# Cross attention with a layer norm on one core: two diagonal Gram blocks packed into one operand, and the keys' mean from one product

## The reference, cut to what matters

```python
# x (4, 2048, 512), ctx (4, 77, 384), all fp32
text_p  = x @ W_text + b_text              # (4, 2048, 512)
audio_p = ctx @ W_audio + b_audio          # (4, 77, 512)
Q = layer_norm(text_p, g1, beta1)
K = layer_norm(audio_p, g2, beta2)
alpha = softmax(Q @ K^T / sqrt(512))
H = (alpha @ audio_p) @ W_out + b_out
out = layer_norm(H + x, g_out, beta_out)
```

## Time and profile before

| what | value |
|---|---|
| median of 3 runs | 277.38 us (276.97 to 277.71) |
| profiled execution, its own time | 277.88 us |
| span of the profiled execution, first to last instruction | 276.2 us |
| mean granted TensorE clock | 0.992 of full |
| busy: PE / DVE / ACT / POOL | 264.3 / 230.8 / 199.1 / 203.4 us |
| share of the chain that ended last: PE / DVE / DMA | 86% / 4% / 3% |

### The profile page before, as it was taken

The page is one execution under the profiler, slowest core; times in us unless marked ns, Lnnn a source line. Parts: engine busy times, 40 slices in busy tenths (PEclk is TensorE's granted clock), DMA queues, the critical chain, the costliest instruction groups (busy, mean ns, idle before and its releaser), DMA issues.

```text
span 276.2 us, 5994 instructions
## 1 busy us (share of the span) xinstructions
PE 264.3 (96%) x1705; PEld 240.3 (87%) x1705; DVE 230.8 (84%) x716; ACT 199.1 (72%) x509; POOL 203.4 (74%) x223
## 2 busy tenths in 40 slices
PE   6799999999999999999999999999999999999980
PEld 6579788999999999999999999999999999999830
DVE  3757889788888888888888888888888888888895
ACT  3584293257888887777777778888888888888881
POOL 5053400113699999999999999999999999999985
PEclk9999999999999999999999999999999999999996
DMA  6919794432244444444444444444444444454116
GB/s 188 285 53 303 277 345 159 120 105 77 77 154 152 157 152 153 154 152 153 152 153 152 152 152 153 153 152 152 152 152 154 153 152 152 152 153 148 81 77 266
DMA packets 21056, 44.03 MB, mean 159 GB/s; under 512 B 2114, under 2 KB 4750, under 8 KB 21034
## 3 DMA queue, kind: packets, MB, share of 16 engines
q1 hardware_dynamic: 20410, 42.74, 45.8%
q10 hardware_dynamic: 624, 1.06, 1.4%
HBM read 21.19 MB, written 16.78 MB: 138 GB/s over the span
## 4 chain that ended last, share of the span: by engine, by line
PE 86%; DVE 4%; DMA 3%; POOL 3%; ACT 2%; issue 1%; SPq 1%; POOLq 0%; ACTq 0%; DVEq 0%
PE psY L1268 44%; PE psO L1280 10%; PE psT L1193 10%; PE psY L1258 7%; DMA zs<-in_ctx_dram 3%; PE psE L1243 2%; PE psE L1244 2%; PE psY L1098 2%; PE psY L1162 1%; PE psT L1131 1%; PE psT L1162 1%; POOL zs L464 1%; POOL zs L460 1%; POOL rstd L452 1%; PE psY L1131 1%
## 5 line engine op out<-in xcount | busy, mean ns | idle before, releaser
L1268 PE MATMUL psY<-proj_hi,x_hi 128*128 128x464 f32 (+3 forms) x256 | 86.1, 336 | 0.0
L1268 PE MATMUL psY<-proj_hi,x_lo 128*128 128x464 f32 (+3 forms) x256 | 83.2, 325 | 0.0
L1268 PE MATMUL psY<-proj_lo,x_hi 128*128 128x464 f32 (+3 forms) x256 | 83.1, 325 | 0.0
L429 POOL TENSOR_TENSOR zs<-zs,shift 128x512 f32<-128x512 f32 x55 | 70.9, 1289 | 4.3
L423 POOL TENSOR_TENSOR zs<-zs,gain 128x512 f32<-128x512 f32 x55 | 71.3, 1296 | 0.9 <-ACT zs L616 0.9
L605 ACT ACTIVATE waste_act<-hid,sc 128x512 bf16<-128x512 f32 x60 | 43.4, 723 | 38.8 <-DVE hid L929 38.8
L435 POOL TENSOR_TENSOR rstd<-stat_eps,neg_half 128x4 f32<-128x4 f32 x30 | 30.5, 1017 | 40.6 <-DVE stat_eps L921 40.6
L1268 PEld LDWEIGHTS psY<-proj_lo,x_hi 128*128 128x128 f32 x256 | 48.5, 189 | 1.5
L1268 PEld LDWEIGHTS psY<-proj_hi,x_lo 128*128 128x128 f32 x256 | 48.3, 189 | 1.6
L1268 PEld LDWEIGHTS psY<-proj_hi,x_hi 128*128 128x128 f32 x256 | 48.4, 189 | 1.5
L909 DVE CUSTOM_DVE_ANT_0 waste_dve<-psY,xs,sums 128x514 bf16<-128x514 f32 x64 | 47.7, 745 | 0.2 <-issue 0.2
(11 more groups left out here) (230 smaller groups left out, 484.4 us busy)
## 6 DMA issues: line engine op xcount, KB each, us to landing
xs<-in_x_dram SPq DMA_DIRECT2D x64, 256.0 KB, 3.0
out_dram<-zs SPq DMA_DIRECT2D x29, 512.0 KB, 3.9
out_dram<-zs SPq DMA_DIRECT2D x6, 256.0 KB, 2.0
xs<-in_L_xattn_W_text_dram SPq DMA_DIRECT2D x4, 256.0 KB, 3.7
xs<-in_L_xattn_W_out_dram SPq DMA_DIRECT2D x2, 512.0 KB, 4.2
wa<-in_L_xattn_W_audio_dram SPq DMA_DIRECT2D x1, 768.0 KB, 7.8
proj_hi<-proj_hi SPq DMA_DIRECT2D x1, 768.0 KB, 8.8
proj_lo<-proj_lo SPq DMA_DIRECT2D x1, 768.0 KB, 10.7
```

What stands on the lines that cost most here:

```text
L429: nc.gpsimd.tensor_tensor(zs[:, q, t, :], zs[:, q, t, :], shift[:], ALU.add).then_inc(out_ready, 1)
L1268: last = nc.tensor.matmul(psY[:, t, to:to + n0], part[:, par, t, k * P:(k + 1) * P], w[:, q, at:at + n0], start=(n == 0), stop=(n == len(P ...
```

## The change

1. **Packing.** For k = 1 and 2 the diagonal 128 x 128 block of the Gram matrix is no longer kept as a full high and a full low block. Its upper triangle, doubled, and the diagonal form one block; its rounded part `pk_hi` stands in place, and its rest `pk_lo` is transposed (by TensorE) and added below the diagonal of the same block in `proj_hi`. In a quadratic form x^T A x a block and its mirror image count the same, so one pass over the block carries high and low part. The pass over `proj_lo` leaves the 128 columns out.
2. **Scaled rows.** So that the diagonal has no rest, each row of the row blocks 1 and 2 is multiplied by r, the rounded diagonal element over the element itself (`rs[:, 0:2]`), and x for these rows by 1/r (`rs[:, 2:4]`). `x_hi` stays the rounded x; `x_lo` becomes psT * (1/r) - `x_hi` for the blocks 1 and 2, so `lo_part` is three instructions instead of one. The score, LIN and NX columns of the two row blocks are scaled too.
3. **The keys' mean.** VectorE sums the four parts of the values (`keys_sum`, three instructions), and TensorE takes one fp32 product of 308 columns instead of eight fp32r ones.
4. **Order.** The Gram rows 1 and 2 are copied from PSUM raw (`t_raw`), and rounded later. `copy_gram(1)` and `copy_gram(2)` move in SyncE's queue from ahead of x of step 2 to behind x of step 3, and wait for the packed block (`pack_ready`) and the right-hand part (`goff_ready`). TensorE waits for both ahead of its loop.

The core of the diff:

```diff
 # SyncE
             def copy_gram(k):
-                at, n = Y_AT[k], D - k * P
                 for buf, made in ((proj_hi, g_hi), (proj_lo, g_lo)):
-                    sp.wait_ge(made, k + 1)
+                    at, n = Y_AT[k], D - k * P
+                    if k in PACKED:
+                        sp.wait_ge(goff_ready, PACKED.index(k) + 1)
+                        sp.wait_ge(pack_ready, PACKED.index(k) + 1)
+                        if buf is proj_lo:
+                            at, n = at + P, n - P
+                    else:
+                        sp.wait_ge(made, 1 if k == 0 else 2)
...
-                            for k in range(1, KD):
-                                copy_gram(k)
+                            copy_gram(KD - 1)
                             sp.wait_ge(wo_ready, KH)
...
                 if isinstance(i, int) and (i, b) == (0, B - 1):
 
+                    for k in PACKED:
+                        copy_gram(k)
                     sp.wait_ge(val_psum, len(KEYS))
 # GpSimd
+            for n, k in enumerate(PACKED):
+                nc.gpsimd.tensor_tensor(pk_lo[n], g_raw[k][:, 0:P], tri, ALU.mult).then_inc(pk_own, 1)
...
 # ScalarE
-            t_hi(1)
+            t_raw(1)
...
-            for k in range(2, KD):
-                t_hi(k)
+            t_raw(2)
+            t_hi(KD - 1)
+            act.wait_ge(dg_ready, 2)
+            nc.scalar.activation(dd[:, 2:4].bitcast(F32R), dd[:, 0:2], ACT.Copy).then_inc(dh_ready, 1)
+            act.wait_ge(rs_ready, 1)
+            act.wait_ge(pk_own, len(PACKED))
+            for n, k in enumerate(PACKED):
+                nc.scalar.activation(pk_hi[n].bitcast(F32R), pk_lo[n], ACT.Copy, scale=rs[:, 4 + n:5 + n]).then_inc(pk_hi_ready, 1)
+            for n, k in enumerate(PACKED):
+                at, w = Y_AT[k] + P, D - (k + 1) * P
+                nc.scalar.activation(proj_hi[:, 0, at:at + w], g_raw[k][:, P:P + w], ACT.Copy,
+                                     scale=rs[:, 4 + n:5 + n]).then_inc(goff_hi_ready, 1)
 # VectorE
+            def keys_sum(k):
+                nc.vector.scalar_tensor_tensor(v_sum, V_BANK[k][:, 0:BS], vec_cols[:, 3 * KH + k:3 * KH + k + 1],
+                                               vT[:, 0, :] if k == 1 else v_sum, ALU.add, ALU.add).then_inc(vsum_ready, 1)
...
             for k in range(KH):
                 keys_lo(k)
+                if k > 0:
+                    keys_sum(k)
                 if k < 2:
                     linear(k)
-            t_lo(1)
             linear(2)
...
-                nc.vector.tensor_tensor(x_lo[:, b % 2, t, :], psT[:], f32(x_hi[:, b % 2, t, :]),
-                                        ALU.subtract).then_inc(x_lo_ready, 1)
+                nc.vector.tensor_tensor(dst[:, 0:KD:KD - 1, :], src[:, 0:KD:KD - 1, :], high[:, 0:KD:KD - 1, :], ALU.subtract)
+                for k in PACKED:
+                    last = nc.vector.scalar_tensor_tensor(dst[:, k, :], src[:, k, :], x_scale[k], high[:, k, :], ALU.mult, ALU.subtract)
+                last.then_inc(x_lo_ready, 1)
...
-            for k in range(2, KD):
-                t_lo(k)
+            for n, k in enumerate(PACKED):
+                nc.vector.tensor_tensor_reduce(out=waste_dve[:, n, 0:P], in0=g_raw[k][:, 0:P], in1=ident[:], scale=1.0, scalar=1e-30,
+                                               op0=ALU.mult, op1=ALU.add, accum_out=dd[:, n:n + 1]).then_inc(dg_ready, 1)
+            t_lo(KD - 1)
             linear(KD - 1)
+            link(nc.vector.reciprocal(rec[:], dd[:]))
+            link(nc.vector.tensor_tensor(rs[:, 0:2], dd[:, 2:4], rec[:, 0:2], ALU.mult))
+            nc.vector.tensor_tensor(rs[:, 2:4], dd[:, 0:2], rec[:, 2:4], ALU.mult)
+            nc.vector.tensor_scalar(rs[:, 4:6], rs[:, 0:2], 2.0, None, ALU.mult)
+            nc.vector.tensor_scalar(rs[:, 6:8], rs[:, 0:2], -1.0 / D, None, ALU.mult).then_inc(rs_ready, 1)
+            dve.wait_ge(rs_ready, 1)
...
+            def diagonal_rest(n):
+                nc.vector.scalar_tensor_tensor(pk_lo[n], pk_lo[n], rs[:, 4 + n:5 + n], pk_hi[n], ALU.mult, ALU.subtract).then_inc(pk_ready, 1)
+            def block_rest(n):
+                nc.vector.scalar_tensor_tensor(proj_lo[:, 0, at:at + w], g_raw[k][:, P:P + w], rs[:, 4 + n:5 + n],
+                                               f32(proj_hi[:, 0, at:at + w]), ALU.mult, ALU.subtract).then_inc(goff_ready, 1)
...
                 nc.vector.scalar_tensor_tensor(kg_lo[:, k, :], kT[:, k, :], g1s[:, k:k + 1], f32(kg_hi[:, k, :]),
                                                ALU.mult, ALU.subtract).then_inc(kg_lo_ready, 1)
+                if k < len(PACKED):
+                    diagonal_rest(k)
+                else:
+                    block_rest(k - len(PACKED))
...
             score_lo(3)
+            dve.wait_ge(pkT_psum, 1)
+            for n, k in enumerate(PACKED):
+                nc.vector.tensor_tensor(proj_hi[:, 0, Y_AT[k]:Y_AT[k] + P], psD[:, n * P:(n + 1) * P], pk_hi[n], ALU.add).then_inc(pack_ready, 1)
 # TensorE
-            for n, (k, v) in enumerate(passes):
-                last = nc.tensor.matmul(A_BANK[0][:, 0:BS], mean_r, v[:, k, :], start=(n == 0), stop=(n == len(passes) - 1))
-            last.then_inc(mean_psum, 1)
+            pe.wait_ge(vsum_ready, KH - 1)
+            nc.tensor.matmul(A_BANK[0][:, 0:BS], mean_of, v_sum, start=True, stop=True).then_inc(mean_psum, 1)
...
+            pe.wait_ge(pk_ready, len(PACKED))
+            for n in range(len(PACKED)):
+                last = nc.tensor.transpose(psD[:, n * P:(n + 1) * P], pk_lo[n], ident[:])
+            last.then_inc(pkT_psum, 1)
             constant(0, C_BANK)
-            pe.wait_ge(lin_lo_ready, KD)
+            pe.wait_ge(lin_lo_ready, KD + len(PACKED))
+            pe.wait_ge(goff_ready, len(PACKED))
+            pe.wait_ge(pack_ready, len(PACKED))
...
+                    if k in PACKED and w is proj_lo:
+                        at, n0, to = at + P, n0 - P, to + P
```

More of the change, by code:

```diff
@@ L146, in cross_attention @@
         krstd = sb("krstd", [P, 4])
+        PACKED = (1, 2)
+        dd, rec, rs = sb("dd", [P, 4]), sb("rec", [P, 4]), sb("rs", [P, 8])
+        lin_r = sb("lin_r", [P, 2])
+        row_scale = {k: rs[:, n:n + 1] for n, k in enumerate(PACKED)}
+        x_scale = {k: rs[:, 2 + n:3 + n] for n, k in enumerate(PACKED)}
         room = [zs[:].rearrange("p b t h -> p (b t h)"), hid[:].rearrange("p c t h -> p (c t h)")]
@@ L163, in cross_attention @@
         mean_of = borrow(1, P)
-        mean_r = kg_hi[:, 0, 0:P]
+        g_raw = {k: borrow(0, D - k * P) for k in PACKED}
+        pk_hi, pk_lo = [borrow(0, P) for _ in PACKED], [borrow(0, P) for _ in PACKED]
+        tri = borrow(1, P)
+        v_sum = kSqSum
         ones = borrow(1, P)
@@ L380, in _ @@
                                     pattern=[[-1, P]], channel_multiplier=1).then_inc(ident_ready, 1)
+            nc.gpsimd.memset(tri, 1.0).then_inc(tri_ready, 1)
+            pool.wait_ge(tri_ready, 1)
+            nc.gpsimd.affine_select(out=tri, in_=tri, compare_op=ALU.is_ge, fill=0.0, base=-1,
+                                    pattern=[[1, P]], channel_multiplier=-1).then_inc(tri_ready, 1)
+            pool.wait_ge(ident_ready, 1)
+            nc.gpsimd.tensor_scalar(pk_lo[0], ident[:], 0.5, 0.0, ALU.mult, ALU.add).then_inc(tri_ready, 1)
+            pool.wait_ge(tri_ready, 3)
+            nc.gpsimd.tensor_tensor(tri, tri, pk_lo[0], ALU.add).then_inc(tri_ready, 1)
             nc.gpsimd.memset(score_c[:, :, S:SC], 0.0).then_inc(extras_ready, 1)
@@ L392, in _ @@
                 at = NX_AT[k]
-                nc.gpsimd.memset(f32(proj_hi[:, :, at:at + 1]), -1.0 / D).then_inc(extras_ready, 1)
+                if k not in PACKED:
+                    nc.gpsimd.memset(f32(proj_hi[:, :, at:at + 1]), -1.0 / D).then_inc(extras_ready, 1)
             def out_lo(k):
@@ L404, in _, with column @@
             pool.wait_ge(lin_ready, KD)
-            pool.wait_ge(extras_ready, 4 + KD)
-            for k in range(KD):
-                at = LIN_AT[k]
-                nc.gpsimd.tensor_copy(proj_hi[:, :, at], lin[:, k:k + 1].to_broadcast([P, B])).then_inc(lin_hi_ready, 1)
-            pool.wait_ge(lin_hi_ready, KD)
-            for k in range(KD):
-                at = LIN_AT[k]
-                nc.gpsimd.tensor_tensor(proj_lo[:, :, at], lin[:, k:k + 1].to_broadcast([P, B]),
+            pool.wait_ge(extras_ready, 4 + KD - len(PACKED))
+            pool.wait_ge(rs_ready, 1)
+            nc.gpsimd.tensor_tensor(lin_r[:], lin[:, 1:3], rs[:, 0:2], ALU.mult).then_inc(lin_r_ready, 1)
+            pool.wait_ge(lin_r_ready, 1)
+            def column(k):
+                return lin_r[:, PACKED.index(k):PACKED.index(k) + 1] if k in PACKED else lin[:, k:k + 1]
+            extra_columns = [(LIN_AT[k], column(k)) for k in range(KD)] + [(NX_AT[k], rs[:, 6 + n:7 + n]) for n, k in enumerate(PACKED)]
+            for at, col in extra_columns:
```

(22 more changed lines are left out.)

35 lines of the change are left out of this document (29 added, 6 removed).

## The result

The changed kernel takes 287.84 us (median of 4 runs, 286.65 to 288.59) against 277.18 us (4 runs): ratio 1.038, 95% interval 1.034 to 1.043. It is slower by 10.7 us. Its profiled execution took 287.59 us with a span of 285.8 us, against 277.88 and 276.2.

A forecast was written before the change was run, and what follows sets the result against it. TensorE, never idle in the loop, was taken as the bound, with VectorE close behind. Step 4 +8.3, two steps after it -0.4, rest 0: +7.9 on 277.88 gives 285.8, or 285.3 on the median; range 280.5 to 288.8.

The forecast's parts named there:

- lo_part and the loop: Loop: lo_part grows 0.25 us a tile to 0.85, VectorE needs 6.80 to 6.86 a step, loop gain nothing.
- Rival 2: Loop: the per-partition scalar costs nothing, TensorE keeps the pace, 0.20 us back per step, -5.6; chance 0.14.
- SyncE's queue: Before step 4: copies (4.0 us) and placements (17.54) wait behind the packed block, delaying x of step 4; transposes +8.3 us.
- Rival 3: SyncE's queue: placements issue quicker, x of step 4 is there at 67.2 to 68, +3 to +3.5 us; chance 0.12.
- The packed block: Ahead of the loop: pack sums done at 48.25 and 48.45 us, transposes of step 1 wait for them, +2.85.
- The tiny chain: Ahead of the loop, VectorE: five tiny instructions, three waited for, 0.6 to 0.9 us, taken as 0.8.
- The keys' mean: Ahead of the loop: one fp32 product (0.52 us) replaces eight (1.14); TensorE and its dependents come 0.5 us earlier.
- the step 4 without the queue: Transposes of step 4 if SyncE's queue did not delay them: 64.38 + 2.85 - 0.6 + up to 0.7, given as 67.2.
- the other steps 0: Loop: steps other than step 4 and the first two after it add 0 us to the sum.
- rival 1: Step 4: the clock falls to 1.2 GHz in the pause, costing 1.7 to 3.3 us, 287 to 288.6; chance 0.22.
- The -0.4 for two steps at TensorE's own pace: Loop: VectorE has run dry at step 4, so the next two steps take TensorE's 6.63 us, -0.4.
- wanted at 54.7: Step 2: copies for k = 1, 2 land by 55 to 56 us, wanted at 54.7, costing up to 0.7.

The follow-up runs named there:

- e2: The changed kernel with lo_part as one plain 512-column subtraction, the scale of x_lo blocks 1 and 2 left out; 284.31 us, ratio 1.023.
- e9: e8 with lo_part as one plain subtraction, the scale of x_lo blocks 1 and 2 left out; 276.33 us, ratio 0.993.
- e5: The changed kernel with the first 7 of SyncE's 21 placements moved ahead of the four copies of the packed Gram rows; 284.50 us, ratio 1.028.
- e8: The changed kernel with the pk_lo transposes ahead of score_weights(2) and the pack sums behind score_lo(0) instead of score_lo(3); 280.88 us, ratio 1.013.
- e11: The changed kernel run once more, unaltered, on another chip; 288.05 us, ratio 1.035.
- e7: The kernel before with only the keys' mean of the change: three sums on VectorE, one fp32 product instead of eight; 277.61 us, ratio 1.002.
- e6: The changed kernel with 14 idle products on TensorE ahead of the wait for x of step 4; 287.84 us, ratio 1.043.

## Why the prediction was right, and where it was off

**Right in mechanism and direction.** The forecast was 285.3, measured 287.84, slower with the chances on that side. +7.9 us was forecast; the medians give +10.7, the two profiled executions +9.7.

- **lo_part and the loop.** 0.85 us forecast, 0.85 measured; VectorE 6.80 to 6.86 forecast, period 6.833; loop gain nothing, shown by e2 and e9 to be VectorE's doing. TensorE's new idle time was put at 0.2 us a step and is 0.21. Rival 2 is out. By the rule of the Trainium skill of about 75 ns beyond the columns for built-in one- and two-source operations (Vector Engine (DVE) Microarchitecture Reference, section 5.2) TensorE would have stayed in front. The scaled pieces cost 0.26 each here, 0.127 beyond 0.133 for their 128 columns. Its slope of 1.04 ns a column agrees with the plain pieces of 512 and 308 columns (0.60 and 0.387 us).
- **SyncE's queue.** Copies 4.0 forecast, 4.39 measured (47.38 to 51.77); placements 17.54 and 17.51; landing 2.9 and 3.10. e5 and e8 show it from both sides. Rival 3 is out: placements did not get quicker.
- **The packed block.** First block done at 48.25 forecast, 47.3 measured; transposes of step 1 at 48.45 and 47.72. All of the difference is there at `diag` already (30.6 and 29.66); from `diag` on, 17.6 us were worked out and came. That difference comes from the start of this execution: the audio projection began 1.3 us earlier than before. Counted from there `diag` is 0.80 us later than before in after, and 0.82 in e11, where +0.45 was forecast. The tiny chain took 0.74 (28.92 to 29.66) for 0.8, and the two diagonal sums 0.42 for 0.56.
- **The keys' mean** was worth -0.5 in the sum and is worth nothing (e7: `diag` 16.29 us behind the audio projection, before 16.26). The fp32 product took 0.76 of busy time behind a wait of 0.41 for VectorE's sums. That is why the forecast has `diag` too early, counted from the audio projection.

**Luck in one number.** The transposes of step 4 were forecast at 72.7 us and came at 72.47. The execution's start took off 1.3 us, and the terms added about as much: the mean 0.5, the copies 0.4, the landing 0.2. In e11 the same kernel has 75.59. Counted from the audio projection, +8.3 was forecast, and +9.4 and +8.7 measured. A slip in the text, without effect: the step 4 without the queue adds up to 67.3, not 67.2.

**Off in size, mostly by one term left out of the sum.** The step is "the other steps 0", with the clock kept apart as rival 1. The clock's fall was no alternative to the forecast: it is what the forecast's own pause does. It happened in step 4 and cost 1.5 us (e6, e5), a little under the 1.7 to 3.3 of rival 1, so 285.3 + 1.5 = 286.8 would have been the sum. The row it was argued from the earlier trace rows already showed the fall behind idle time. By the Trainium skill, TensorE: Matmul & The Clock Gate, Part 1, an idle array closes the gate; this trace agrees, with 0.50 behind a wait of 2.85 us. The -0.4 for two steps at TensorE's own pace is not there either (188.09 in e6, with the pause and a full clock). With that, with the clock and with the 0.4 to 1.1 us at step 4 the forecast's +7.9 becomes 10.2 to 10.9.

**Off twice with little effect.** The wait for the copies in step 2 was 1.72 us where up to 0.7 was counted in "wanted at 54.7": the last copy landed at 55.9, inside the forecast's 55 to 56, but was wanted at 54.2 already. It and the low clock behind it made the pause in step 4 2.9 us and not 5. Step 4's start did not move, as the queue sets it. And with VectorE out of the way a step takes 6.68 us on average (e2, e9) where 6.63 stood for TensorE alone. The starts agree with the 99 ns a tile (464 columns 0.210, 336 0.153, 208 0.107 from start to start with proj_lo, so 0.103), and every second step of e9 does take 6.63. In the others TensorE waits 0.04 to 0.15 us for ScalarE's `parts_t`, an engine that the forecast gave room.

**What stays open.** Why copies issued by GpSimd land late: they and SyncE's placements were in flight together and both took longer, but no run had the copies alone. That `mix` waits for `parts_t` is read from the traces; no run moved ScalarE's order to test it. And the median of e6 does not show the 1.5 us of the clock.

## What to carry to other kernels

Price a faster operand format by everything it asks of the second-busiest engine: here 0.10 us a tile saved on TensorE needed 0.25 on VectorE, which had about 0.24 free, and the gain was zero. Before a step moves in an in-order transfer queue, write down what stands behind it and when that is wanted; 7 of the 11 us went by moving two groups of instructions forward. Whenever a forecast contains a pause of TensorE, add the clock to the same sum, not to a rival. And before two profiles are compared by absolute times, count both from an instruction that stands ahead of the change: here single executions began 1.3 to 3.8 us apart, and an agreement to 0.2 us was chance.
